# Packing of queries, keys and values moved from transfers to ScalarE, with sums over 128 rows, in a small audio tower

## What is computed

```python
# 1: nine-tap convolution, scaled by the norm of its window, tanh, bias, relu
conv = conv_general_dilated(x, kernel[9, 64, 128])          # 742 tokens out
h = relu(tanh(|conv * scale|) * sign + bias)
# 2: linear attention, 8 heads of 16, with a decay per head
q, k, v = split(layernorm(h) @ Wqkv + bqkv, 3)
q = (elu(q) + 1) / 4;  k = elu(k) + 1
memory = cumsum(k_dec outer v, over tokens);  k_sum = cumsum(k_dec)
out = (q_dec @ memory) / (q_dec . k_sum + 1e-5)
h = h + layernorm(out @ Wout + bout) * gamma + beta
# 3: 32 experts, each takes its top 371 tokens by router probability
y[idx] += prob * (silu(tokens @ W_up[group] + b_up) @ W_down[e] + b_down)
h = h + y
```

## Time and profile before

| | us |
|---|---|
| median of 3 runs | 1230.74 |
| lowest, highest | 1227.21, 1232.94 |
| the profiled execution | 1221.58 |
| its span, first to last instruction | 1219.6 |
| PE busy | 945.5 |
| DVE busy | 668.7 |
| ACT busy | 381.3 |
| POOL busy | 381.6 |

### The profile page before, as it was taken

The page is one execution under the profiler, slowest core; times in us unless marked ns, Lnnn a source line. Parts: engine busy times, 40 slices in busy tenths (PEclk is TensorE's granted clock), DMA queues, the critical chain, the costliest instruction groups (busy, mean ns, idle before and its releaser), DMA issues.

```text
span 1219.6 us, 21893 instructions
## 1 busy us (share of the span) xinstructions
PE 945.5 (78%) x6489; PEld 754.6 (62%) x6489; DVE 668.7 (55%) x2137; ACT 381.3 (31%) x778; POOL 381.6 (31%) x338
## 2 busy tenths in 40 slices
PE   5498999999999999999999988200277677676772
PEld 4377788788787787777878867100155555555552
DVE  5354775676675676576667656588633233232320
ACT  0321332332432332333234232566332222222221
POOL 7020121121011011011111100000157777777775
PEclk9688988989998898898999878555578778787877
DMA  2112212212302302312230220100134444444432
GB/s 69 31 30 59 57 49 74 75 31 73 88 23 66 88 26 71 81 39 63 75 85 24 69 69 31 30 0 0 42 71 79 77 78 81 73 78 75 76 64 27
DMA packets 117085, 70.07 MB, mean 57 GB/s; under 512 B 40448, under 2 KB 113408, under 8 KB 117024
## 3 DMA queue, kind: packets, MB, share of 16 engines
q1 hardware_dynamic: 97568, 55.68, 17.1%
q0 software_dynamic: 19456, 13.74, 8.2%
HBM read 29.86 MB, written 20.23 MB: 41 GB/s over the span
## 4 chain that ended last, share of the span: by engine, by line
PE 44%; issue 15%; SPq 14%; POOL 10%; DMA 8%; DVE 7%; ACT 1%; DVEq 0%; POOLq 0%; ACTq 0%
SPq L394 12%; PE ps L807 8%; POOL out_dram L576 5%; PE pst L822 5%; PE po L844 5%; PE pa L755 4%; DMA f<-token_rows,idx 4%; PE po L928 3%; PE pc L868 3%; POOL f L566 3%; PE po L835 3%; DMA kd<-f 3%; PE pa L781 2%; SPq L400 2%; PE pa L757 2%
## 5 line engine op out<-in xcount | busy, mean ns | idle before, releaser
L576 POOL DMA_INDIRECT out_dram<-tqk,idx x96 | 154.1, 1605 | 48.6 <-issue 39.3
L807 PE MATMUL ps<-qb,kd 128*128 128x256 f32 x384 | 124.3, 452 | 37.7 <-DMA kd<-f 27.0
L566 POOL DMA_INDIRECT f<-token_rows,idx x96 | 96.1, 1001 | 85.9 <-issue 76.9
L755 PE MATMUL pa<-wc,xT 128*128 128x128 f32 x768 | 116.3, 297 | 6.6 <-DMA wc<-in_L_tok_kernel_dram 6.0
L928 PE MATMUL po<-qb 114*128 114x128 f32 (+1 forms) x576 | 111.6, 349 | 6.1 <-ACT qb L709 6.1
L755 PEld LDWEIGHTS pa<-wc,xT 128*128 128x128 f32 x768 | 97.7, 199 | 18.5 <-issue 9.1
L807 PEld LDWEIGHTS ps<-qb,kd 128*128 128x128 f32 x384 | 74.2, 215 | 55.4 <-issue 44.3
L530 POOL TENSOR_TENSOR wnorm<-wnorm,expo 128x6 f32<-128x6 f32 x16 | 21.1, 1321 | 278.3 <-DVE wnorm L1021 256.9
L928 PEld LDWEIGHTS po<-qb 114*128 114x128 f32 (+1 forms) x576 | 98.0, 250 | 9.2 <-ACT qb L709 7.8
L844 PEld LDWEIGHTS po<-vm,P 128*64 128x64 f32 x1536 | 103.7, 139 | 0.0
L844 PE MATMUL po<-vm,P 128*64 128x34 f32 x1536 | 103.5, 223 | 0.0
(11 more groups left out here) (230 smaller groups left out, 1964.7 us busy)
## 6 DMA issues: line engine op xcount, KB each, us to landing
token_rows<-row SPq DMA_DIRECT2D x16, 480.0 KB, 4.1
xT<-in_x_cols_dram SPq DMA_DIRECT2D x17, 388.0 KB, 4.3
vm<-sv SPq DMA_DIRECT2D x32, 204.0 KB, 3.5
qb<-f SPq DMA_DIRECT2D x256, 24.0 KB, 1.9
kd<-f SPq DMA_DIRECT2D x64, 96.0 KB, 2.4
out_dram<-h SPq DMA_DIRECT2D x16, 384.0 KB, 2.8
kd<-in_L_ffn_W_up_dram SPq DMA_DIRECT2D x32, 170.5 KB
qb<-in_L_ffn_W_down_dram SPq DMA_DIRECT2D x32, 114.0 KB
```

Source lines behind the costliest of these rows:

```text
L566: eng.indirect_dma_start(out=xg[0:n, e.par, t, :], out_offset=None, in_=rows[:, :], in_offset=bass.IndirectOffsetOnAxis(ap=idx[0:n, e.k, t ...
L576: eng.indirect_dma_start(out=out_rows, out_offset=bass.IndirectOffsetOnAxis(ap=idx[0:n, e.k, t:t + 1], axis=0), in_=yw[0:n, e.par, t, :], ...
L755: eng.matmul(dst, xT[:, b.par, a:a + C], wc[:, t, :], start=(t == 0), stop=False)
L807: mm = eng.matmul(ps[c % 2][:, pack * 4 * HC:(pack + 1) * 4 * HC], kd[:, b.par, pack, c, :, :].rearrange("p u t -> p (u t)"), qb[:, b.par, ...
```

## The change

Three things, and a new list. (1) `qb`, `kd` and `vm` are written by ScalarE copies. A mask `turn_of` (one column for each head position, made by POOL at the start) is the scale of four copies for each half, so `qb` needs no zeroing. The copies are items of a new stage K that works on batch b-1, in the pass that uses them: `dq0`, `dk`, `dv`, `dq1`. All three buffers have a new layout, in which score matmul `u` of a chunk takes one sub-chunk's keys and queries for all eight heads. (2) `kt` has two slots per chunk with the other sub-chunk's rows zero, so T contracts over 128 rows, and its copy is two ACT instructions of 64 rows. (3) The ninth tap's weights get 64 zero rows and contract over 128 rows. The memset of `qb` goes, and memsets of `kt` (POOL) and of 64 rows of `wc` (DVE) come.

```diff
-        ORDER = [("A", "ts"), ("C", "o0"), ("A", "conv0"), ("T", 0), ("S", 0), ("A", "sq"), ("A", "win"), ("T", 1),
-                 ("C", "w0"), ("A", "w"), ("T", 2), ("A", "x"), ("C", "o1"), ("C", "z0"), ("T", 3), ("C", "out"),
...
+        ORDER = [("A", "ts"), ("A", "sq"), ("C", "o0"), ("A", "conv0"), ("K", "dq0"), ("C", "o1"), ("T", 0),
+                 ("K", "dk"), ("C", "w0"), ("C", "z0"), ("C", "out"), ("T", 1), ("C", "w1"), ("C", "z1"),
+                 ("A", "w"), ("A", "win"), ("T", 2), ("C", "s0"), ("C", "s1"), ("A", "x"), ("C", "zq0"),
+                 ("C", "zq1"), ("S", 0), ("T", 3), ("A", "scale"), ("K", "dv"), ("S", 1), ("C", "zg0"),
...
-                if (stage, what) == ("A", "dq"):
-                    if first(b):
-                        eng.wait_ge(S["zero_done"], 3)
-                    hold(eng, "f_done", b.count(4, 2))
-                    hold(eng, "s_ps", b.count(NC, NC, back=2))
-                    for h in range(H):
-                        g, j = h // 4, h % 4
-                        own = slice(E * h, E * h + E)
-                        for u in range(2):
-                            eng.dma_start(qb[own, b.par, u ^ g, j, :], f[own, b.par, 0, u, :]).then_inc(qb_in[b.par], 16)
...
+            eng.memset(kt[:, :, :, :, :], 0.0).then_inc(S["zero_done"], 1)
...
+            step(eng.memset(head_of[:, :], 1.0))
...
+            step(eng.tensor_tensor(turn_of[:, :], head_of[:, 0:4], head_of[:, 4:8], ALU.add))
...
-                    eng.activation(kt[:, b.par, lo:hi, :], pa[half][:, 0:(hi - lo) * D].rearrange("p (c d) -> p c d", d=D),
-                                   ACT.Copy).then_inc(S["kt_sb"], 1)
+                    for u in range(2):
+                        own = slice(HC * u, HC * u + HC)
+                        eng.activation(kt[own, b.par, lo:hi, u, :], pa[half][own, 0:(hi - lo) * D].rearrange("p (c d) -> p c d", d=D),
+                                       ACT.Copy).then_inc(S["kt_sb"], 1)
+                if stage == "K" and what in ("dq0", "dq1"):
...
+                    need(eng, "f_done", b.count(4, half + 1))
+                    need(eng, "s_ps", b.count(NC, HALF[half][1], back=2))
+                    for j in range(4):
+                        ins = eng.activation(qb[:, b.par, j, cols], f[:, b.par, 0, cols], ACT.Copy, scale=turn_of[:, j:j + 1])
+                    ins.then_inc(S["qb_done"], 1)
+                if (stage, what) == ("K", "dk"):
...
+                    for g in range(2):
+                        own = slice(64 * g, 64 * g + 64)
+                        ins = eng.activation(kd[own, b.par, :, :, g, :].rearrange("p c u t -> p (c u) t"),
+                                             f[own, b.par, 1, :].rearrange("p (n t) -> p n t", t=HC), ACT.Copy)
+                    ins.then_inc(S["kd_done"], 1)
+                if (stage, what) == ("K", "dv"):
...
+                    for g in range(2):
+                        for u in range(2):
+                            ins = eng.activation(vm[64 * g:64 * g + 64, b.par, u, :, g, :],
+                                                 sv[HC * u:HC * u + HC, b.par, :, 4 * g:4 * g + 4, :].rearrange("p c h e -> p c (h e)"),
+                                                 ACT.Copy)
+                    ins.then_inc(S["vm_done"], 1)
...
-                        mm = eng.matmul(dst, xT[CIN:128, b.par, a:a + C], wc[CIN:128, 4, :], start=False, stop=True)
+                        mm = eng.matmul(dst, xT[:, b.par, a:a + C], wc[:, 4, :], start=False, stop=True)
...
+                    if c in (0, HALF[1][0]):
+                        need(eng, "qb_done", b.count(2, 2 if c else 1))
                     if c == 0:
-                        need(eng, qb_in[b.par], b.m * 256 + 256)
-                        need(eng, kd_in[b.par], b.m * 64 + 64)
+                        need(eng, "kd_done", b.count(1, 1))
...
-                    eng.matmul(pst[:, 0:H * E1], kt[own, b.par, c, :], sv[own, b.par, c, :, :].rearrange("p h e -> p (h e)"),
+                    eng.matmul(pst[:, 0:H * E1], kt[:, b.par, c, u, :], sv[:, b.par, c, :, :].rearrange("p h e -> p (h e)"),
...
-            eng.memset(qb[:, :, :, :, :], 0.0).then_inc(S["zero_done"], 1)
             eng.memset(tsum[:, NC:NC + 1], 0.0).then_inc(S["decays_done"], 1)
+            eng.memset(wc[0:CIN, 4, :], 0.0).then_inc(S["wc_zero"], 1)
```

More of the change, by code:

```diff
@@ L281, in iteration @@
                 before = Batch(M, 0) if p else Batch(M - 1, 1)
-                batch = {"A": Batch(M, p), "S": before, "T": before, "V": before, "C": Batch(M - 1, p)}
+                batch = {"A": Batch(M, p), "K": before, "S": before, "T": before, "V": before, "C": Batch(M - 1, p)}
                 for stage, what in ORDER:
-                    if {"A": a, "S": b, "T": b, "V": b, "C": c}[stage]:
+                    if {"A": a, "K": b, "S": b, "T": b, "V": b, "C": c}[stage]:
                         part(stage, what, batch[stage])
@@ L384, in part @@
                     load_x(ahead)
-                if (stage, what) == ("A", "dq"):
-                    if first(b):
-                        eng.wait_ge(S["zero_done"], 3)
-                    hold(eng, "f_done", b.count(4, 2))
-                    hold(eng, "s_ps", b.count(NC, NC, back=2))
-                    for h in range(H):
-                        g, j = h // 4, h % 4
-                        own = slice(E * h, E * h + E)
-                        for u in range(2):
-                            eng.dma_start(qb[own, b.par, u ^ g, j, :], f[own, b.par, 0, u, :]).then_inc(qb_in[b.par], 16)
[L395 to L401, removed]
-                if (stage, what) == ("A", "dv"):
-                    hold(eng, "vs_done", b.count(1, 1))
-                    hold(eng, "o_ps", b.count(NC, NC, back=2))
-                    for u in range(2):
-                        own = slice(HC * u, HC * u + HC)
-                        eng.dma_start(vm[own, b.par, :, u, :], sv[own, b.par, :, :, :].rearrange("p c h e -> p c (h e)")
-                                      ).then_inc(vm_in[b.par], 16)
                 if (stage, what) == ("C", "out"):
@@ new lines, in part @@
+                if stage == "K" and what in ("dq0", "dq1"):
+                    half = int(what[-1])
+                    cols = slice(half * QH, half * QH + QH)
+                    if first(b) and half == 0:
+                        eng.wait_ge(S["consts_pool"], ATTENTION_CONSTS)
+                    need(eng, "f_done", b.count(4, half + 1))
[3 more added lines that the diff above has]
+                    ins.then_inc(S["qb_done"], 1)
@@ new lines, in part @@
+                if (stage, what) == ("K", "dk"):
+                    if first(b):
+                        eng.wait_ge(S["zero_done"], 3)
+                    need(eng, "f_done", b.count(4, 4))
+                    need(eng, "s_ps", b.count(NC, NC, back=2))
+                    for g in range(2):
[3 more added lines that the diff above has]
+                    ins.then_inc(S["kd_done"], 1)
@@ new lines, in part @@
+                if (stage, what) == ("K", "dv"):
+                    if first(b):
+                        eng.wait_ge(S["zero_done"], 3)
+                    need(eng, "vs_done", b.count(1, 1))
+                    need(eng, "o_ps", b.count(NC, NC, back=2))
+                    for g in range(2):
[4 more added lines that the diff above has]
+                    ins.then_inc(S["vm_done"], 1)
@@ L737, in part @@
                     need(eng, "tsum_done", b.count(1, 1))
-                    need(eng, "kt_sb", b.count(2, 2, back=1))
+                    need(eng, "kt_sb", b.count(4, 4, back=1))
                     eng.matmul(pa[1][:, WIN:WIN + NC], band[:, 0, :], tsum[:, 0:NC], start=True, stop=False, skip_group_check=True)
@@ L745, in part @@
                         eng.wait_ge(S["wc_in"], 16 * 3)
+                        eng.wait_ge(S["wc_zero"], 1)
                     need(eng, x_in[b.par], b.m * 16 + 16)
-                    need(eng, "kt_sb", b.count(2, half + 1, back=1))
+                    need(eng, "kt_sb", b.count(4, 2 * half + 2, back=1))
                     if half:
@@ L813, in part @@
                     c, u = k // 2, k % 2
-                    own = slice(HC * u, HC * u + HC)
                     if k == 0:
-                        need(eng, "kt_sb", b.count(2, 2))
+                        need(eng, "kt_sb", b.count(4, 4))
                         need(eng, "vs_done", b.count(1, 1))
@@ L1074, in part @@
                     cols = slice(u * QH, u * QH + QH)
[L1075 removed]
+                    need(eng, "kd_done" if w else "qb_done", b.count(1, 1, back=2) if w else b.count(2, u + 1, back=2))
                     need(eng, "kt_ps" if w else "o_ps", b.count(2, 2, back=2) if w else b.count(NC, NC, back=2))
@@ L1084, in part @@
                     need(eng, "st_ps", b.count(TK, TK, back=2))
-                    need(eng, "o_ps", b.count(NC, NC, back=2))
+                    need(eng, "vm_done", b.count(1, 1, back=2))
```

77 lines of the change are left out of this document (40 added, 37 removed), and 18 rows, old and new, of the table ORDER.

## The result

The changed kernel takes 1088.39 us (median of 4, 1086.71 to 1091.49) against 1231.84 before in the same comparison, a ratio of 0.885 with a 95% interval of 0.881 to 0.889. Where one execution of a kernel took over 1.5% more than its fastest, the median without it is given beside the median of all; here that is 1230.74 before.

What follows compares the result with a forecast made beforehand. PE bounds the pipelined phase, with waits for SP's transfer queue and a resulting half clock. Periods save 84.8 us, start 1.1, end 2: 87.9 off the profiled 1221.58 gives 1133.7, plus 2.3: 1136 us, range 1112 to 1174 (own range 1112 to 1155).

Steps and rivals of the forecast that it cites:

- The wait and the half clock: Pipelined periods: PE's 1.6 us wait for transfers ahead of S 0 and the 2.9 us clock fall both go.
- ACT's price and place: ScalarE's new copies cost 8.2 us a batch, bounds 6.5 to three times as much; dk ends 0.6 us ahead of S 0.
- Rival D: ACT's copies, dk behind oT and dq0, hold S 0; at four times the price 1280 us, slower than before; chance 3%.
- The short waits: PE's small waits in the new list, for hnT, fk1 and state copies: 1.1 us a period, bounds 0 to 3.
- Rival A: Small waits between coupled PE, DVE and ACT eat the gain, 2 us more each period: 1166 us; chance 14%.
- PE's list is then 39.7 - 2.1 = 37.6: PE's work a period at full clock: 128 rows save 0.8 us on ninth taps and 1.3 on T.
- 1.09 us or 0.27 for each matmul: Ninth-tap price: four full 128-row matmuls of a convolution chunk, compared with 0.41 us for the 64-row tap.
- For the last batch I take 2 us less: Last pass of the pipelined phase, without stage A: the end gains 2 us.
- The scale: Profiled execution stood 9.2 us below the median; 1133.7 us by its scale, plus 2.3 us, made the forecast.
- The start: Up to the first S 0: begins near 59.5 us in place of 60.6, a gain of 1.1 us.
- B: Rival: the half clock has another cause than the 1.6 us wait and stays, 41 us come back: 1177; chance 8%.
- C: Rival: 64-row matmuls' longer distance is their place in the stream and stays, 15 x 2.1 = 32 us: 1168; chance 5%.

Runs made afterwards that it cites:

- E9: The changed kernel with the item list of the kernel before and with ninth taps and state sums T back over 64 rows, so only the copies are left: 1159.56 us.
- E8: The changed kernel with the item list of the kernel before (dq0 and dk ahead of T 0, dv behind x, dq1 ahead of V 0): 1108.76 us.
- E5: The kernel before with 8 of its 16 query transfers left out for each batch, four heads' queries never packed: 1160.25 us.
- E3: The changed kernel with both the ninth taps and the state sums T back over 64 rows, new list kept: 1180.75 us.
- E2: The changed kernel with the state sums T back over 64 rows, two key slots kept: 1141.16 us.
- E4: The kernel before with ninth tap and T over 128 rows, its transfers and list kept: 1214.59 us, ratio 0.987.
- E6: The changed kernel with dk as 24 copies of 64 columns in place of 2 of 768: 1120.3 us.
- E12: The changed kernel with its ninth taps over 64 rows, the three of a half grouped behind its twelve full matmuls: 1089.49 us.
- E1: The changed kernel with its ninth tap back over 64 rows, nothing else: 1111.58 us.
- E7: The changed kernel with dk as 48 copies of 32 columns in place of 2 of 768: 1184.27 us.

## Why the prediction was right, and where it was wrong

The runs give a ledger of the three parts, in one order:

| | us | mean period |
|---|---|---|
| before | 1231.8 | 44.2 |
| copies for transfers (E9) | 1159.6 | 40.2 |
| and 128 rows (E8) | 1108.8 | 36.95 |
| and the new list (after) | 1088.4 | 36.2 |

- **The wait and the half clock: right.** Forecast 1.6 and 2.9 us a period, 44.2 to 39.7 without them. E9 and E5 have undisturbed periods of 39.9 and 39.7 to 39.8, and their means of 40.2 and 40.3 give 4 us of the 4.5. With the sum's 1.1 us of short waits, 15 periods without the rows' term would be 609.8 us; E9 has 603.0, 6.8 less.
- **ACT's price and place: right.** 8.2 us a period was forecast; the windows give 23.5 less 14.8, 8.7. `dk` was to end 0.6 us ahead of S 0 and ends 0.5 ahead. Rival D had its place right and did not come.
- **The short waits: right.** 1.1 us was taken; 0.56 in each period and 0.52 in every other one are the large ones. Rival A did not come.
- **"PE's list is then 39.7 - 2.1 = 37.6": the term that was mis-sized.** The term for the 64-row matmuls was 2.1 us, bounded by 0.8 + 1.7 = 2.5 above; it is 3.0 in undisturbed periods with the old list (E9 to E8), though a wait of 0.6 us opens ahead of S 0, and 4.1 with the new (E3 against the changed kernel). The step that failed stands in "1.09 us or 0.27 for each matmul": I took the full matmuls between two taps as undisturbed and compared the tap with them. They were paying for the change of mode themselves; undisturbed, a full matmul is 0.22 to 0.23. The same for T, where the scores behind it go from 0.97 to 0.86. Every price from a neighbour was too high, so each saving came out too small. Over the 15 periods E9 to E8 is 48.8 us where the term gave 31.5, so 17.3 of the periods' 35.3 us are this term; by the new list it would be near 30. The list's 0.75 us a period (E8), which I had at nothing, is 11.2, and the 6.8 above are the rest.
- **"For the last batch I take 2 us less": 10.7 short.** With the old list (E8) the last pass is at 0.77 of the clock and the end is 10.8 us longer; with the new list and T over 64 rows (E2) it is 10.5 longer. So it takes both, and I had put a price on neither there.
- **The scale.** The profiled execution of before was 9.2 us below its median, of which I gave back 2.3; that of after is 3.1 above its own. That is 5.4 of the 47.6 us; by spans the miss is 41.9.
- **The start: 0.8 short.** S 0 at 60.3, forecast 59.5.
- **Rivals B and C** fell. B by E5, for the kernel before. E9 shows the same with all transfers replaced and the matmuls as they were. C (rows are free) has a true half: the rows are free, the changes between them are not.

The gain is also not the sum of its parts. 128 rows are worth 51 us once the transfers are gone (E9 to E8) and 15 (4 to 27) while they are there (E4). That follows from the queue, which takes 15.6 us from `fq1` to S 0 in the steady periods before the change, and 15.6 and some 16.3 by turns in those of E4: what PE saves ahead of `fq1` shortens the period, what it saves behind goes into the wait. That E4 gained 0.7 us a period and not 2.6 goes mostly to the longer half clock, some 1.5 us by the estimate there, and for some 0.4 us to this stretch, which is longer in every other period.

**What stays open.** What brings the half clock in the traced execution of E3, with the new list, 64 rows and no wait over 0.4 us, and not in E9, with the old list. The new list puts transposes over 64 rows, T and taps next to each other around the convolution; that this is the cause is a guess. Open too is why E6's waits of 0.8 to 1.6 us are mostly spared it.

## What to carry to other kernels

When you price a matmul of another row count, don't take its neighbours in the same stretch as the undisturbed ones: look for a run of equal matmuls far from any change, since a change from 128 to 64 rows and back costs 0.3 to 0.4 us here, and it lands on the matmuls on both sides. Zero rows that keep all matmuls alike cost nothing here. Grouping the odd ones leaves one such change for each group, 0.28 us, and comes out free in E12 only because one of its two groups stands beside other 64-row matmuls. And where a queue or a wait bounds a period, take it away before you shorten the engine that waits, or the saving will be a longer wait, here with a lower clock on top.

## What the hardware did that I had not expected

- Full matmuls between 64-row ones take 0.27 us each and 0.22 to 0.23 in a stretch without (E1, E12, the changed kernel).
- 64-row taps and 64-row transposes next to each other take turns and cost less than apart: E12's half beside the transposes takes 3.89 us against 4.22 with all taps over 128 rows.
- TensorE fell to half its clock while it waited for nothing (the longest execution of E3, 432 to 450 us, granted 0.53 with PE busy throughout).
- Waits of like length came with unlike clocks: 1.6 us with the half clock in 13 of 15 periods (before), 0.8 to 1.6 us with two of 15 periods lengthened by it (E6), 2.8 to 3.8 us with all (E7), and 0.5 to 0.6 us with none (E8, all but its last period).
- 64-row copies on ScalarE cost the same whether they cross the partition halves or not: of `dv`'s four copies of 408 columns two cross, and all take 0.53 to 0.54 us; `dk`, which doesn't cross, takes 0.84 for 768.
